# Stacked queries and keys in DRAM, fewer and larger transfers per batch and piece, and a PSUM copy moved to VectorE

## The reference

```python
qh = (q @ Wq.T + bq).reshape(B, QN, H, DH).transpose(0, 2, 1, 3)
kh = (k @ Wk.T + bk).reshape(B, KN, H, DH).transpose(0, 2, 1, 3)
vh = (v @ Wv.T + bv).reshape(B, KN, H, DH).transpose(0, 2, 1, 3)
qh = layernorm(qh, q_gamma, q_beta) * scale
kh = layernorm(kh, k_gamma, k_beta)
attn = jax.nn.softmax(jnp.einsum('bhqd,bhkd->bhqk', qh, kh), axis=-1)
x = jnp.einsum('bhqk,bhkd->bhqd', attn, vh)
return x.transpose(0, 2, 1, 3).reshape(B, QN, E) @ Wp.T + bp
```

## Time and profile before

| | us |
|---|---|
| median of 3 runs | 1444.58 (1439.33 to 1449.13) |
| the profiled execution | 1436.91 |
| its span | 1435.1 |
| mean granted clock of TensorE | 0.924 of full speed |
| qkv phase, from the start to the first QK | 151.0 |
| first QK to the last (unit 63) | 151.0 to 359.05 |

### The profile page before, as it was taken

How to read it: one execution, slowest core, us unless ns; L and a number is a source line. 1 busy time by engine, 2 the same in 40 slices (tenths; PEclk the granted TensorE clock), 3 DMA queues, 4 the chain that set the end, 5 groups by cost and what they waited for, 6 DMA issues and landing times. The chain is left out here.

```text
span 1435.1 us, 27993 instructions
## 1 busy us (share of the span) xinstructions
PE 1270.8 (89%) x7093; PEld 995.2 (69%) x7094; DVE 838.1 (58%) x2027; ACT 648.6 (45%) x1350; POOL 728.7 (51%) x963
## 2 busy tenths in 40 slices
PE   7876779999887999999999499847999999969997
PEld 4554447667655888888888377624888888857776
DVE  5753236556584777777777588694333333346665
ACT  3544347767523545455554277635433333321110
POOL 2332236566502565555655366404655555267775
PEclk9986579999998999999999699957999999989999
DMA  3487486885352556555555588554555556774443
GB/s 105 115 197 159 132 224 193 234 216 173 123 236 87 172 156 164 165 158 171 155 170 147 183 255 226 158 234 148 174 162 161 162 161 157 136 226 131 129 134 115
DMA packets 157086, 240.44 MB, mean 168 GB/s; under 512 B 34812, under 2 KB 122125, under 8 KB 152144
## 3 DMA queue, kind: packets, MB, share of 16 engines
q1 hardware_dynamic: 134584, 173.48, 41.8%
q0 software_dynamic: 20640, 56.39, 14.1%
q10 hardware_dynamic: 1784, 9.66, 1.7%
HBM read 164.41 MB, written 70.55 MB: 164 GB/s over the span
## 5 line engine op out<-in xcount | busy, mean ns | idle before, releaser
L1346 POOL DMA_INDIRECT xg<-t_xn,token x160 | 151.3, 945 | 156.8 <-PE psum L2246 69.2
L2322 POOL DMA_INDIRECT su_yg<-t_y,slot x128 | 122.9, 960 | 67.5 <-issue 38.7
L2258 PE MATMUL psum<-gu,m_xT 128*128 x640 | 153.2, 383 | 0.0
L2217 DVE TENSOR_TENSOR m_h<-psum,m_sg 128x256 f32<-128x256 f32 x80 | 34.0, 425 | 158.7 <-ACT m_sg L2196 158.7
L2258 PEld LDWEIGHTS psum<-gu,m_xT 128*128 128x128 f32 x640 | 116.6, 192 | 12.9
L1599 PE MATMUL psum<-w,m_xT_high 128*128 x284 | 118.6, 418 | 0.0
L1621 PE MATMUL psum<-m_both,m_hT_high 128*128 128x512 f32 x284 | 111.3, 414 | 1.4 <-DVE top_i L1565 1.2
L1599 PE MATMUL psum<-w_low,m_xT_high 128*128 x284 | 112.3, 396 | 0.0
L1599 PE MATMUL psum<-w,m_xT_low 128*128 x284 | 112.3, 395 | 0.0
L1472 POOL DMA_INDIRECT t_y<-top_v,dest x36 | 67.7, 1880 | 69.3 <-DVE top_v L1565 66.9
L1546 DVE TENSOR_TENSOR m_both<-w,m_both 128x1024 fp32r<-128x1024 f32 x71 | 87.0, 1225 | 17.2 <-ACT m_both L1514 17.1
(11 more groups left out here) (312 smaller groups left out, 3390.1 us busy)
## 6 DMA issues: line engine op xcount, KB each, us to landing
w<-in_w SPq DMA_DIRECT2D x71, 512.0 KB, 3.8
t_y<-m_y SPq DMA_DIRECT2D x80, 256.0 KB, 2.2
q<-t_q_high SPq DMA_DIRECT2D x32, 256.0 KB, 4.2
w<-in_w SPq DMA_DIRECT2D x8, 1024.0 KB, 5.3
t_w_low<-at_low SPq DMA_DIRECT2D x64, 128.0 KB, 2.4
t_x<-at_x SPq DMA_DIRECT2D x64, 128.0 KB, 2.1
w_low<-t_w_low SPq DMA_DIRECT2D x8, 1024.0 KB, 11.8
at_yg<-t_y SPq DMA_DIRECT2D x32, 256.0 KB, 3.5
```

The source lines that it names most:

```text
L1346: pool.indirect_dma_start(out=g.xg1[j % GB][:, k * D:(k + 1) * D], out_offset=None, in_=g.xn4, in_offset=bass.IndirectOffsetOnAxis(ap=g.to ...
L2258: last = pe.matmul(ps_gu[p][:, k * 2 * M1:(k + 1) * 2 * M1], xT[p][:, at:at + P], g.gu[:, bass.ds(ex[k] * (DC * 2 * M1) + c * 2 * M1, 2 * ...
L2322: pool.indirect_dma_start(out=yg[p][k][:, :], out_offset=None, in_=g.y1, in_offset=bass.IndirectOffsetOnAxis(ap=g.slot[:, at:at + 1], axis ...
```

## The change

- The scratch in DRAM is one array for q and one for k, `q_parts` and `k_parts`, with high and low as the outermost dimension, in the order in which the tiles have them; heads stand in another order within a tile (`pair_at`), and what reads them is adapted.
- A k tile holds zeros for the other head of a pair. They were written once by POOL; now ACT writes them, with a gain and bias masked by head, so that `affine` of a k piece has 4 passes in place of 2, each still of 308 columns, and `part` handles 616 columns in place of 308.
- A q piece is stored by 2 DMAs (before: 8), a k piece by 4 (before: 2, of half the bytes). A batch is loaded by 4 DMAs (before: 9). One of them reads q's high part twice by a source with a step of 0 over 2 copies.
- In the attention mT goes by 1 DMA in place of 2, low chunks are stored two at a time with 2 sides of two chunks in place of 4 of one, and the 12 loads of u = 12 are spread over the halves from u = 12 to u = 23.
- The copy of the value products out of PSUM goes from ACT to DVE.

```diff
     def affine(self, act, i, s_passed):
 
-        p, n = i.mod(2), 2 * DC * self.rows
+        p, r = i.mod(2), self.rows
         wait(act, self.s_low, i.shift(-1).n)
-        wait(act, self.st[p], i.div(2).n * self.landed)
+        wait(act, self.st[p], i.div(2).n * 32 * self.copies)
         wait_alone(act, self.s_t, i.n + 1, s_passed)
         for out in (self.full, self.high):
-            last = act.activation(out[p], self.ps_t[:, 0:n], ACT.Identity, bias=self.beta, scale=self.gamma)
+            for m in range(self.copies):
+                last = act.activation(out[p].rearrange("p (n m r) -> p n m r", m=self.copies, r=r)[:, :, m, :],
+                                      self.ps_t[:, 0:2 * DC * r].rearrange("p (n r) -> p n r", r=r), ACT.Identity,
+                                      bias=self.beta[m], scale=self.gamma[m])
         last.then_inc(self.s_out, 1)
...
-            for first, last in self.store_rows:
-                sp.dma_start(self.stored[which](i.n, first, last),
-                             rows[first:last, :].bitcast(F32).rearrange("p (c t) -> p c t", c=DC)).then_inc(self.st[p], 16)
-
-
-QK_LOADS, QK_RING = 9, 4
-Q_ROWS = [(i * 2 * DH, (i + 1) * 2 * DH) for i in range(P // (2 * DH))]
-Q_STORES = 2 * len(Q_ROWS)
-
-
-def query_rows(part):
-
-    return lambda b, first, last: part.rearrange("r b (c m) t -> m r b c t", c=DC)[first // (2 * DH)][:, b, :, :]
-
-
-def key_rows(part):
-
-    return lambda i, first, last: part.rearrange("(c p) k -> p c k", p=P)[:, :, i * 2 * LK:(i + 1) * 2 * LK]
+            n = self.stored.shape[4]
+            each = rows.shape[1] // n
+            for a in range(each):
+                sp.dma_start(self.stored[which].rearrange("r b m n -> m r b n")[:, :, i.n * each + a, :],
+                             rows[:, a * n:(a + 1) * n].bitcast(F32)).then_inc(self.st[p], 16)
...
+QK_LOADS, QK_RING = 4, 4
+Q_COLS, K_COLS = DC * SQ, DC * 2 * LK
+
+
+def pair_at(h):
+
+    return h % (HG // DC) * DC + h // (HG // DC)
...
 def load_queries_keys(sp, g, b, slot):
 
     landed = g.s_qk[slot]
-    for j, part in enumerate((0, 0, 1)):
-        sp.dma_start(g.q3[slot][32 * j:32 * j + 32, :].bitcast(F32).rearrange("p (h t) -> p h t", h=HG),
-                     g.q_parts[part][:, b, :, :]).then_inc(landed, 16)
-    for j, part in enumerate((0, 1, 0)):
-        for a in range(2):
-            at = 32 * j + DH * a
-            sp.dma_start(
-                g.k3[slot][at:at + DH, :].bitcast(F32).rearrange("p (h a k) -> p h a k", h=HG, a=2)[:, :, a, :],
-                g.k_parts[part].rearrange("(h a p) k -> a p h k", a=2, p=DH)[a][:, :, b * LK:(b + 1) * LK])\
-                .then_inc(landed, 16)
+
+    queries, keys = (parts[:, :, b, :, :].rearrange("w r m n -> w r (m n)") for parts in (g.q_parts, g.k_parts))
+    high_twice = queries[0:1, :, :].broadcast_to([2, 2 * DH, HG * SQ])
+    for dst, src in ((g.q3[slot][0:64, :], high_twice), (g.q3[slot][64:96, :], queries[1, :, :]),
+                     (g.k3[slot][0:64, :], keys), (g.k3[slot][64:96, :], keys[0, :, :])):
+        sp.dma_start(dst.bitcast(F32), src).then_inc(landed, 16)
...
+                    sp.dma_start(g.q3[b.mod(QK_RING)][96:98, :].bitcast(F32)
+                                 .rearrange("p (m c t) -> p m c t", c=DC, t=SQ)[:, :, gr, :],
+                                 mT[gr][96:96 + HG, :].bitcast(F32)).then_inc(s_mr[gr], 16)
...
-                if i is not None:
+                if i is not None and i.mod(2) == 1:
                     sp.wait_ge(w_low, i.n + 1)
-                    sp.dma_start(g.w13_low_d[:, bass.ds(i.n * CHUNK, CHUNK)], low[i.mod(4)][:, :].bitcast(F32))\
-                        .then_inc(low_st[i.mod(4)], 16)
+                    sp.dma_start(g.w13_low_d[:, bass.ds((i.n - 1) * CHUNK, 2 * CHUNK)], low[i.n // 2 % 2][:, :].bitcast(F32))\
+                        .then_inc(low_st[i.n // 2 % 2], 16)
...
+                if 12 <= u.off < 12 + len(later):
+                    dst, src = later[u.off - 12]
+                    sp.dma_start(dst[:, :], src).then_inc(s_next, 16)
...
+                    side, half = i.mod(4) // 2, i.mod(2)
+                    if half == 0:
+                        wait_alone(pool, low_st[side], i.div(4).n * 16, passed[1])
...
+                v = unit_at(u, T_PV + 1)
+                if v is not None and v.mod(2) == 1:
+                    b, side = v.div(4), v.mod(4) // 2
+                    dve.wait_ge(pv_mm, v.n + 1)
+
+                    wait(dve, raw_t, b.shift(-1).n * 2)
+                    dve.tensor_copy(oraw[b.mod(2)][:, side * 4 * P:(side + 1) * 4 * P], ps_raw)\
+                        .then_inc(raw_out, 1)
...
-        ("q_high", (2 * DH, NB, HG, SQ)), ("q_low", (2 * DH, NB, HG, SQ)), ("k_high", (D, NB * LK)), ("k_low", (D, NB * LK)))}
+        ("q_parts", (2, 2 * DH, NB, HG // DC, Q_COLS)), ("k_parts", (2, 2 * DH, NB, HG // DC, K_COLS)))}
```

More of the change, by code:

```diff
@@ L237, in transpose @@
             for c in range(DC):
-                last = pe.transpose(self.ps_t[:, (c * 2 + a) * r:(c * 2 + a + 1) * r],
+                at = (c * 2 + a if self.pairs else a * DC + c) * r
+                last = pe.transpose(self.ps_t[:, at:at + r],
                                     self.n[p][0:r, (a * DC + c) * P:(a * DC + c + 1) * P], self.g.ident[0:r, 0:r])
@@ L331, in qkv_phase @@
         passed = [sem(f"passed_{n}") for n in ("dve", "pool", "act")]
-        g.s_qk, s_neg, s_zero = [sem(f"s_qk{i}") for i in range(QK_RING)], sem("s_neg"), sem("s_zero")
-        neg = g.w2[:, 6 * W2_COLS:6 * W2_COLS + HG * 2 * LK]
+        g.s_qk, s_neg = [sem(f"s_qk{i}") for i in range(QK_RING)], sem("s_neg")
+        neg = g.w13[:, CONTEXT_COLS + 8 * D:CONTEXT_COLS + 8 * D + HG * 2 * LK]
         ps_p, ps_t, ps_xt, ps_v = g.bank[0:4], g.bank[4], g.bank[5:7], g.bank[7]
[L335 to L338, removed]
+        k = HeadNorm(sb, sem, g, "k", LK, wk, ones3, bias3[:, 0:D], [masked[:, 2 * a:2 * a + 1] for a in range(2)],
+                     [masked[:, 2 * a + 1:2 * a + 2] for a in range(2)], eps, ps_p, ps_t, k_split, g.k_parts, False)
+        q = HeadNorm(sb, sem, g, "q", P, wq, ones3, bias3[:, D:2 * D], [scaled[:, 0:1]], [scaled[:, 1:2]], eps, ps_p, ps_t,
+                     q_split, g.q_parts, True)
         g.q_st = q.st
@@ L446, in _ @@
             center(2, heads_of(wq[:, :]), wmean[:, 1, :], P, DC * H, s_w)
-            dve.wait_ge(s_rest, 4 * 16)
+            dve.wait_ge(s_rest, 5 * 16)
             dve.tensor_scalar(scaled[:, :], gb[:, 0:2], float(DH) ** -0.5, None, ALU.mult).then_inc(s_gs, 1)
+            for a in range(2):
+                dve.tensor_scalar(masked[:, 2 * a:2 * a + 2], gb[:, 2:4], of_head[:, a:a + 1], None, ALU.mult)\
+                    .then_inc(s_gs, 1)
             dve.wait_ge(s_v1, 1)
@@ L599, in attention0_phase @@
         high = [sb(f"high{i}", [P, CHUNK], F32R) for i in range(2)]
-        low = [sb(f"low{i}", [P, CHUNK], F32R) for i in range(4)]
+        low = [sb(f"low{i}", [P, 2 * CHUNK], F32R) for i in range(2)]
         s_w, s_next, w_high, w_low, w_back = (sem(n) for n in ("s_w", "s_next", "w_high", "w_low", "w_back"))
         s_x, x1_st, xn_st, s_w13, s_mr = ([sem(f"{n}{i}") for i in range(2)] for n in ("s_x", "x1_st", "xn_st", "s_w13", "s_mr"))
-        low_st = [sem(f"low_st{i}") for i in range(4)]
+        low_st = [sem(f"low_st{i}") for i in range(2)]
         v_ready = sem("v_ready")
@@ L744, in half @@
                 if i is not None:
-                    wait_alone(pool, low_st[i.mod(4)], i.div(4).n * 16, passed[1])
+                    side, half = i.mod(4) // 2, i.mod(2)
+                    if half == 0:
+                        wait_alone(pool, low_st[side], i.div(4).n * 16, passed[1])
                     pool.wait_ge(w_high, i.n + 1)
-                    pool.tensor_tensor(low[i.mod(4)][:, :], chunk(i), high[i.mod(2)][:, :], ALU.subtract).then_inc(w_low, 1)
+                    pool.tensor_tensor(low[side][:, half * CHUNK:(half + 1) * CHUNK], chunk(i), high[i.mod(2)][:, :], ALU.subtract).then_inc(w_low, 1)
                     wait_alone(pool, w_low, i.n + 1, passed[1])
@@ L818, in half @@
             def half(u):
-                v = unit_at(u, T_PV + 1)
-                if v is not None and v.mod(2) == 1:
-                    b, side = v.div(4), v.mod(4) // 2
-                    act.wait_ge(pv_mm, v.n + 1)
-                    wait(act, raw_t, b.shift(-1).n * 2)
-                    act.activation(oraw[b.mod(2)][:, side * 4 * P:(side + 1) * 4 * P], ps_raw, ACT.Copy)\
-                        .then_inc(raw_out, 1)
                 v = unit_at(u, T_ST)
@@ L2400, in __init__ @@
             scratch[n] for n in ("xn", "xn4", "y0", "y1", "beta", "w13_low"))
-        self.q_parts, self.k_parts = ([scratch[n + part] for part in ("_high", "_low")] for n in ("q", "k"))
+        self.q_parts, self.k_parts = scratch["q_parts"], scratch["k_parts"]
 def program(nc, dram_in, out, scratch):
```

61 lines of the change are left out of this document (27 added, 34 removed).

## The result

The changed kernel takes 1617.96 us (median of 4 runs, 1609.7 to 1622.79) against 1441.95 us before (1432.19 to 1449.13): a ratio of 1.122, 95% interval 1.1132 to 1.1308. The forecast was 1598, range 1510 to 1665. The profiled execution has a span of 1620.2 us, 185.1 more than before.

A forecast was written before the change was run, and what follows sets the result against it. It took SP's DMA issues to bound qkv, PE's work plus stalls behind batch loads the attention, and few engines per transfer to decide afterwards. 1436.9 + 70 + 88 = 1595; with medians 7.7 higher it said 1598, range 1510 to 1665.

The forecast's parts named there:

- The engines of a transfer: All DMAs: outermost count is dealt evenly over as many engines as divide it, at most 16; the same engines each time.
- lowest engine: DMA queue: the engine taken to share all confined transfers; 194 us of work in qkv, 16.2 us per attention batch.
- qkv, +70: qkv phase: confined stores and preloads fill the shared engines, first QK at 221 us in place of 151.
- The attention, +88: Attention, units 9 to 57: twelve batches take 254 us in place of 166.5, 21.2 us each.
- a chain from the low store through POOL, ACT and SP: Attention: low store lands late behind batch loads, POOL, ACT and SP wait in turn, next loads late; 21.2 us a batch.
- rival 4: Attention: the queue's work alone bounds it, the chain is hidden; +28, total 1535 us; within the forecast's range, no separate chance.
- the sum of 1595: Whole kernel: profiled execution 1436.9 us plus 70 for qkv plus 88 for the attention.
- Smaller edits at nothing: Attention: raw copy on DVE taken as 0 (0 to 2 us), the 12 spread loads as 0 (at most +6).
- Rival 2: Only the load of two copies is confined, not the stores: qkv +11, attention +88, 1536 us; chance 0.05.
- Rival 3: Only the stores are confined: QK at 184 us, qkv +33, attention -20, total 1450 us; chance 0.03.
- rival 1: All transfers still use 16 engines: qkv -17, attention 144 us in place of 166.5, total 1400 us; chance 0.10.
- the prediction's upper bound: Attention: +115 if PE falls to half its clock in the gaps and 2 us of it join the chain.

The follow-up runs named there:

- stack_padded: stack_merged plus one unused DRAM row behind q's 32 rows of each part, so the 64-row q load starts with outermost count 2; 1610.58 us, ratio 1.1183.
- stack_merged: Changed kernel with the parts paired otherwise in the q and k tiles, so q's 64-row load has outermost count 64; 1505.71 us, ratio 1.0466.
- store_rows: Changed kernel with another DRAM order, so stores write 128 rows; q's high part still loaded from a source of 2 copies, by four loads; 1545.81 us, ratio 1.0659.
- load_split: Changed kernel with the two-copy load of q's high part split into two loads of 32 rows, stores unchanged; 1501.35 us, ratio 1.0374.
- stores_by_two: Changed kernel with each q store cut into two of 64 rows, outermost count 2 in place of 4; 1702.0 us, ratio 1.1832.
- low_first: Changed kernel with only the low store moved ahead of expert weights and batch loads in SP's half; 1613.84 us, ratio 1.1184.
- before_copies: Kernel before the change with one edit: q's high part loaded once, as 64 rows from a source of 2 copies; 1580.47 us, ratio 1.0941.
- both_spread: Changed kernel with stores of 128 rows and six loads of 32 rows per batch, no large transfer with a small outermost count; 1449.86 us, ratio 1.0043.
- spread_four_sides: both_spread with low chunks as before the change: four sides of one chunk, one store per chunk; 1420.45 us, ratio 0.9839.

## Why the prediction was right, and where its steps were off

**The engines of a transfer.** Right, and shown: stack_padded and stack_merged for the count of 2, store_rows and load_split for 4 against 128, stores_by_two for the same engines each time. The shares of 12.5%, 12.4% and 25.6% give the number directly. The first of them belongs to a load with a source of two copies, the second to one that reads nothing twice. The closing packets that the prediction counts in the earlier trace rows show again: from 208 to 222 us the changed kernel has 617 packets of data and 18 of under 512 B in q1, one to 34, where 32 rows of a store on each of four engines give one to 32. Only the counts of these runs and of the earlier trace rows are seen, so the rule for any count is my conclusion alone. Nor does any trace say which of the 16 engines a transfer uses: the "lowest engine" of the recorded sums stands for the engines that the confined transfers share, and what is shown of it is that they meet on the same ones (stores_by_two, 13.1%, first QK 76.4 us later).

**qkv, +70.** Measured +78. The step's middle price, 24 GB/s an engine, held within that (91 GB/s on four engines are 22.7 each); the transposes of q pieces during the preloads came 23.9 us per two pieces (135.33, 159.25 us), and two pieces' stores, two loads of x and a preload had been summed to 2 x 5.5 + 2 x 0.61 + 11.65 = 23.9. The load's 9.75 us is right here: in the preload issued at 129.37 its 8 KB packets take 0.31 us each, 32 on each of the two engines. (The stretch of SP's queue that is shown for the kernel before has 26 DMAs, not 25.) Split by part: with the stores alone confined the first QK is at 195.2, with the load alone at 167.2, with neither at 133.0.

**The attention, +88.** Measured +87 from unit 9 to 57, but the step behind it failed: it let a chain from the low store through POOL, ACT and SP make 21 us out of 16.2 us of work. low_first takes that wait away and the time stays. Part of what replaces it is work that I had sized too small: the load of two copies, 9.75 us in the sum. In the stall shown above, the expert load is issued at 408.20 and the low store behind the loads lands at 430.98, 22.4 us after the end of that issue; take off 2.4 for the expert, 1.9 and 0.6 for the other loads and the store, 1.7 of latency, and 15.8 are left. The trace's packets say the same: on the two engines 8 KB packets follow each other from 412.5 to 427.95, 15.4 us. They take 0.5 to 0.9 us each up to 418, while the other engines work, and mostly 0.31 from 420 on. It is not so in every batch. The next load, issued at 426.67, starts only at 431.5, when the others' shares have moved, and each of the two engines needs 10.7 us for it. Of the 12 loads from 252 to 506 us six take 14 to 16 us and six about 11.

With 13.1 us as the mean in place of 10.4 (34 packets, two of them of the next load, at 0.31) a batch is 16.2 + 2.7 = 18.9 us of work on the two engines of the load, against 253.8 / 12 = 21.2 measured. So rival 4's mechanism (the queue's work alone), with a larger price for the load, explains most of the time, and the +88 came out right partly by luck: a chain that is not needed made up for a load that was priced too low. For the last 2 us a batch the cause is not shown. One candidate is a chain through mT, which I priced at nothing of its own: it is held by the same queue and lands in the same moment as the low store, PE waits for it, and the next batch's loads wait for PE's last ST. Why the packets take longer while other engines work is open too; no run separates it.

**The end of the attention.** I stopped the sum at unit 57. The loads of u = 53 stall unit 58 as well, and units 57 to 63 took 18.6 us more. That, and 8 in qkv, is what the sum of 1595 is short of the profiled execution's 1622. The last step of the sum was wrong by itself: 1595 and 7.7 are 1603, not 1598.

**Smaller edits at nothing.** For the copy on DVE no run contradicts it. The low stores in pairs stood in the chain, without a price of their own. In the changed kernel none can be seen (before_copies, with four sides, takes 254.7 us from unit 9 to 57, the changed kernel 253.8), but they cost 19 to 29 us (both_spread against spread_four_sides) once the transfers are spread. The 12 loads over 12 halves were not tried alone.

**The rivals.** Rival 2's 1536 was 1546 in store_rows. Rival 3's 1450 was 1501 in load_split, rival 1's 1400 was 1450 in both_spread: both had let the attention's stalls go with the load. In both_spread units 9 to 57 take 184.3 us where rival 1 had 144; the pairs of low chunks are 14.6 of these 40, and the other 26 are stalls that the kernel before has as well (169.7 with four sides, 166.5 before). In load_split 11 of the 51 lie in qkv, where the first QK was put at 184 and came at 195.2. That SP was what ended last in qkv is right, the first QK at 133 us shows it.

## What to carry to other kernels

In this kernel fewer and larger transfers paid only where the outermost count of both sides kept all DMA engines in use: with stores of 4 and a load of 2 the ratio was 1.122, with stores of 128 and loads of 32 it was 1.0043, and 0.9802 with four low sides, the low store first and k's loads later. So read the shape of each transfer before counting how many there are, and look for a low DMA share (here 0.33 and 0.50, against 0.74 in both stretches of the earlier trace rows and 0.85 and 0.75 in both_spread, from 75 to 133 and 156 to 340 us) with everybody waiting on DMAs. Such a transfer also delayed what was queued behind it, here a store and an 8 KB copy that had nothing to do with it: both landed some 20 us after their issue. Where a buffer's stores are paired, look at what stands ahead of the pair in the queue.

## What the hardware showed that was not expected

- With a transfer on few engines in the queue the issuing engine was held up too. ACT's copy of mT had ended at 416.52 when SP began to issue mT at 416.54, and that issue took 5.48 us in place of 0.65 five us earlier. In both_spread no single issue from 156 to 340 us takes over 2.4 us. What SP waits for in such an issue no run shows.
- The stall shown above cost more than its length on PE. PE's granted clock was 0.61 over it, 0.58 in the ten us behind it, in which PE was busy all the time, and 1.00 after that; unit 42 takes 442.60 - 436.69 = 5.9 us there, where such a half takes 3.3 once the clock is at 1.00 (452.62 to 455.97). In the kernel before it was 0.50 from 140 to 151 us, the half clock that the prediction's upper bound takes; in this stall it was 0.65 from 418.5 to 428.5 us and 0.50 from 431 to 437.

```profile
417.00:437.00 20.00, 5.77 (x28) 3.62 (x27) 2.18 (x7) 3.00 (x6) 5.04 (x11) 0.61 0.39 126
437.00:447.00 10.00, 10.00 (x56) 7.38 (x55) 4.21 (x11) 4.28 (x8) 3.68 (x8) 0.58 0.29 105
447.00:458.00 11.00, 11.00 (x95) 8.22 (x93) 7.75 (x22) 7.35 (x13) 7.88 (x17) 1.00 0.62 186
```
